# Second value head stored with its two batches exchanged, and PSUM regrouped into one quad of banks, in a gated delta rule kernel

## The chip, the cores and the metric

The kernel runs on one core of one Trainium2 chip, as one launch. The metric is the device time in microseconds (us). A core has TensorE (PE: matmuls, and PEld: its weight loads), VectorE (DVE), ScalarE (ACT), GpSimd (POOL) and DMA queues, of which SyncE (SP) issues most. Engines run their own instruction streams and meet at semaphores.

## The reference

Two independent parts. A small one (a ternary-quantised feed-forward step on tokens) is done in the first 470 us and isn't touched. The large one, cut to what matters:

```python
# x: (8, 512, 256); 16 key heads (HK), 32 value heads (HV), two value heads per key head; width 128; chunks of 64 tokens
q, k, v, z = split(x @ W_qkvz)                      # per key head: q 128, k 128, v 2*128, z 2*128
q, k, v = silu(causal_conv1d([q, k, v], 4 taps))
# per value head: g cumulative decay within a chunk, A = -(beta k) k^T * exp(g_i - g_j), strictly lower
attn = (I - A)^-1                                    # _correct_row, done by rows in the reference
value_corrected = attn @ (v * beta);  k_cumdecay = attn @ (k * beta * exp(g))
for c in range(8):                                   # chunks
    v_prime = value_corrected[c] - k_cumdecay[c] @ state
    out[c] = (q_c @ state) * exp(g) + tril(q_c k_c^T * decay) @ v_prime
    state = state * exp(g_last) + (k_c * k_decay)^T @ v_prime
y = rmsnorm(out * silu(z)) @ W_out
```

## The kernel before

Batches are taken two at a time (NB = 2, four pairs), and for each pair the 16 key heads in turn: 64 steps, called heads here, numbered g. A head carries its two value heads (h = 0, 1) together. A tile of 128 partitions is 64 tokens of batch 0 above 64 tokens of batch 1 (`half(b)`), so a product of one batch's chunk uses a quarter of TensorE's array: rows `half(b)` by columns `half(b)`, given by `tile_position`.

The kernel is a software pipeline written by hand. `core` of head g walks its 8 chunks (c = 0..7), and into it `weave` sets the 24 pieces of `front` of head g+1 (`front_piece`, s = 0..23, three per chunk). Each engine has its own version of both, and the order in them is the order of issue. On TensorE one chunk is `core_step`: `key_state` (state times keys), `query_state`, `out_project` of chunk c-3, `output_rows` (transposes of chunk c-2), piece 3c, `solve` (inverse times residual), piece 3c+1, `update` (state products), `intra`, piece 3c+2. ScalarE copies `solve`'s result to `ww`, VectorE forms `residual` and `update_state` (four scalar_tensor_tensor of 128x128), `gate_out` multiplies by silu(z).

The front projects the next head through a ring of two PSUM banks (`pj`), in the order k, k, z, q, q, v0, z, v0, k transposed (kt) twice, v1, v1, z, z, v transposed (vt) four times. `fill_ring(n)` on TensorE waits until `pcopy` says that entry n-2 has been emptied by ScalarE's `empty_ring`. So the second q (n = 4, in piece 5) waits for the first z (n = 2). Behind that second q stand, in piece 5, `square_sums` (L673) and `chunk_squares` (L687). The inverse is made by small blocks: VectorE inverts 16x16 blocks (`invert_rows` to `join_right`), DMAs put them in place (`dd`, `ee` and, for the second head's turned half, `eturn`), TensorE does `off_products` and three `fixpoint` rounds of 64x64 products, ScalarE negates (`negated`), VectorE adds (`add_round`).

PSUM has the banks pj0, pj1, ms0, ms1 (front), `dsb` (two banks: state products, transposed rows, output projection), `pot` (key_state and solve) and `pod` (query_state and intra).

## Time and profile before

| | us |
|---|---|
| median of 3 runs | 4962.62 (4961.70 to 4965.15) |
| the profiled execution | 4955.99 |
| its span, first to last instruction | 4954.2 |
| TensorE busy | 4628.7 (93%) |
| VectorE busy | 3573.7 (72%) |
| ScalarE busy | 3072.0 (62%) |
| GpSimd busy | 694.4 (14%) |
| mean granted TensorE clock | 0.986 |

The profile is one execution. Its parts are the busy times, the span in 40 slices, the queues, the chain that ended last, the groups of instructions by line, and the DMA issues. Further views are asked of the same trace: a timeline (instructions of one engine in order, neighbours of the same line merged, start and length in us, with idle time and its releaser in brackets), groups by line and shape, and sums by stretch. The matmuls' ends are modelled and overlap the next start, so the time that a group of matmuls holds TensorE is read from its start to the next group's start. A float32 product shows as two MATMUL records, a transpose as one.

### The profile page before, as it was taken

Reading aid. Unit: us, or ns where it says so; the run is one execution under the profiler, and the core shown is the slowest. Engines: PE = TensorE matmul, PEld = TensorE weight load, DVE = VectorE, ACT = ScalarE, POOL = GpSimd, SP = SyncE. Lnnn points to the kernel's source line nnn. Section 1 sums busy time; section 2 is a strip of 40 time slices with the busy share of each in tenths; the row PEclk is TensorE's granted clock in tenths of the full one; section 3 lists DMA queues with packets and bytes.
Section 4 is the critical chain, followed back from the end, with each engine's and each line's share of the span. In section 5 each row is a group of like instructions: output and inputs, shape, how many; then the busy total and the mean of one; then the engine's idle time right before and its main releaser. Section 6 shows DMA issues by size and latency. Waiting matters only on the chain.

```text
span 4954.2 us, 144941 instructions
## 1 busy us (share of the span) xinstructions
PE 4628.7 (93%) x54288; PEld 3167.2 (64%) x54320; DVE 3573.7 (72%) x7576; ACT 3072.0 (62%) x7979; POOL 694.4 (14%) x680
## 2 busy tenths in 40 slices
PE   4998999999999899999999899999999899999998
PEld 2555666666666566666666566666666666666666
DVE  7554677777777677777777677777777677777776
ACT  2333666666666566666666566666666566666665
POOL 0000111111111111111111111111111111111111
PEclk8999999999999999999999999999999999999999
DMA  2111222222223222222223222222223222222221
GB/s 61 41 35 63 63 69 55 60 66 61 68 56 77 66 69 53 61 66 61 69 50 79 69 61 56 65 66 62 56 60 82 68 59 58 64 67 61 69 59 34
DMA packets 760100, 305.22 MB, mean 62 GB/s; under 512 B 672880, under 2 KB 716016, under 8 KB 749168
## 3 DMA queue, kind: packets, MB, share of 16 engines
q1 hardware_dynamic: 620144, 287.40, 23.5%
q10 hardware_dynamic: 139264, 8.42, 1.8%
q8 instruction: 455, 7.45, 0.6%
q14 instruction: 237, 1.94, 0.1%
HBM read 216.96 MB, written 66.07 MB: 57 GB/s over the span
## 4 chain that ended last, share of the span: by engine, by line
issue 56%; PE 27%; POOL 8%; DVE 4%; ACT 2%; DMA 1%; SPq 1%; POOLq 0%; DVEq 0%; ACTq 0%
PE pj L660 5%; POOL rout L1559 4%; PE dsb L819 3%; PE pj L655 2%; POOL gb L1550 2%; POOL kn L1555 2%; PE pot L605 2%; PE dsb L791 1%; PE pot L777 1%; PE ms L693 1%; PE pod L803 1%; PE ms L589 1%; PE pot L748 1%; PE pj L589 1%; PE pod L760 1%
## 5 line engine op out<-in xcount | busy, mean ns | idle before, releaser
L660 PE MATMUL pj<-xnT,wt 128*128 128x512 f32 x2048 | 1022.2, 622 | 34.0 <-DMA cw<-in_L_attn_conv_weight 20.6
L1292 DVE SCALAR_TENSOR_TENSOR cy<-xpad,cw,cy 128x1024 f32<-128x1024 f32 x768 | 976.2, 1278 | 7.9 <-ACT cy L1003 0.9
L1559 POOL TENSOR_TENSOR rout<-rin,expo 128x2 f32<-128x2 f32 x512 | 358.3, 700 | 3737.4 <-DVE rin L1443 3737.4
L1429 DVE SCALAR_TENSOR_TENSOR st<-st,gel,dsb 128x128 f32<-128x128 f32 x1536 | 430.9, 343 | 288.0 <-PE dsb L791 285.1
L819 PE MATMUL dsb<-wo,yT 128*128 128x256 f32 x2048 | 575.0, 403 | 13.2 <-issue 12.1
L660 PEld LDWEIGHTS pj<-xnT,wt 128*128 128x128 f32 x2048 | 351.7, 191 | 363.8 <-issue 349.0
L1002 ACT ACTIVATE xpad<-pj 128x512 f32<-128x512 f32 x512 | 305.5, 597 | 359.1 <-PE pj L660 359.1
L655 PE MATMUL pj<-wt,xnT 128*128 128x256 f32 x2048 | 509.9, 392 | 0.0
L1062 ACT ACTIVATE yT<-dsb 128x256 f32<-128x256 f32 x512 | 203.2, 397 | 469.0 <-PE dsb L810 467.5
L819 PEld LDWEIGHTS dsb<-wo,yT 128*128 128x128 f32 x2048 | 348.0, 189 | 117.8 <-issue 89.6
L655 PEld LDWEIGHTS pj<-wt,xnT 128*128 128x128 f32 x2048 | 368.3, 189 | 84.6 <-issue 44.3
L791 PEld LDWEIGHTS dsb<-ww,arena 64*128 64x128 f32 x3584 | 234.9, 186 | 274.0 <-issue 269.9
L994 ACT ACTIVATE arena<-pj 128x512 f32<-128x512 f32 x256 | 153.1, 598 | 392.2 <-issue 247.8
L1057 ACT ACTIVATE arena<-arena,rout 128x128 f32<-128x128 f32 x1024 | 352.6, 395 | 59.0 <-POOL rout L1559 55.7
L1416 DVE SCALAR_TENSOR_TENSOR rr<-pot,nge,arena 128x128 f32<-128x128 f32 x896 | 270.5, 343 | 115.8 <-PE pot L748 115.8
L1051 ACT ACTIVATE junk<-arena 128x128 f32<-128x128 f32 x1024 | 315.3, 324 | 57.2 <-DVE arena L1439 49.9
L1003 ACT ACTIVATE cy<-pj,cw 128x512 f32<-128x512 f32 x512 | 350.2, 684 | 0.0
L803 PE MATMUL pod<-ww,arena 64*64 64x128 f32 x4096 | 334.9, 281 | 13.7 <-ACT ww L1045 10.4
L791 PE MATMUL dsb<-ww,arena 64*128 64x128 f32 x3584 | 320.5, 297 | 8.3 <-issue 4.2
L777 PE MATMUL pot<-rr,bda 64*64 64x128 f32 x3584 | 293.5, 282 | 19.0 <-DVE rr L1416 19.0
L748 PE MATMUL pot<-st,kq 128*64 128x256 f32 x1792 | 289.8, 398 | 6.1 <-DVE st L1429 4.6
L760 PE MATMUL pod<-st,qge 128*64 128x128 f32 x3584 | 276.9, 273 | 3.2 <-issue 3.2
(174 smaller groups left out, 8009.7 us busy)
## 6 DMA issues: line engine op xcount, KB each, us to landing
qge<-ge_rows SPq DMA_DIRECT2D x64, 1024.0 KB, 7.1
wt<-in_L_attn_W_qkvz SPq DMA_DIRECT2D x64, 768.0 KB
gb<-g_rows SPq DMA_DIRECT2D x128, 256.0 KB
a_d<-at SPq DMA_DIRECT2D x64, 512.0 KB, 2.6
wo<-in_L_attn_W_out SPq DMA_DIRECT2D x64, 256.0 KB, 2.7
x_d<-xpair SPq DMA_DIRECT2D x128, 128.0 KB, 1.8
ap_<-a_d SPq DMA_DIRECT2D x512, 16.0 KB, 1.8
dd<-x_d SPq DMA_DIRECT2D x512, 16.0 KB, 2.1
```

Of the source, the lines that this page charges most:

```text
L655: last = mm(pj[n % 2][:, v * GRP * DH:(v + 1) * GRP * DH], xnT[:, k, c * P:(c + 1) * P], wt[:, k, 4 * DH:4 * DH + GRP * DH], start=(k == 0 ...
L660: last = mm(pj[n % 2][:, :], wt[:, k, col:col + DH], batch(xnT, k, i), start=(k == 0), stop=(k == KD - 1))
L748: last = mm(pkw[half(b), 0:GRP * DH], kq[:, p, c, b, :], st[:, c % 2, b, :, :].rearrange("p h d -> p (h d)"), start=True, stop=True, tile_ ...
L777: last = mm(pkw[half(b), (GRP + h) * DH:(GRP + h + 1) * DH], bda[half(b), p, c * GRP + h, :], rhs, start=True, stop=True, tile_position=(b ...
L791: last = mm(dsb[:, b, h * DH:(h + 1) * DH], kkd[p][half(b), c * GRP + h, :], ww[half(b), h, :], start=True, stop=True, tile_position=(b * ...
L803: last = mm(po[half(b), h * DH:(h + 1) * DH], it[half(b), p, c * GRP + h, :], ww[half(b), h, :], start=(c == 0), stop=True, skip_group_che ...
L819: last = mm(dsb[:, 0, GRP * DH:GRP * DH + D], yT[:, h, :], wo[:, p, h, :], start=(h == 0), stop=(h == GRP - 1))
L1003: last = fn(cy[:, m % 2, i, :], src[:, :], ACT.Copy, scale=cw[:, m, TAPS - 1:TAPS])
L1057: last = fn(zz[p][:, j, h, :], zz[p][:, j, h, :], ACT.Copy, scale=rout[:, h:h + 1])
L1292: stt(y, x[:, :, tap:tap + SEQ], cw[:, kind, tap:tap + 1], y, ALU.mult, ALU.add).then_inc(S["conv"], 1)
L1429: last = stt(st[:, (c + 1) % 2, b, h, :], st[:, c % 2, b, h, :], gel[:, p, h, b * NC + c:b * NC + c + 1], dsb[:, b, h * DH:(h + 1) * DH], ...
L1559: tt(rout[:, :], rin[:, :], expo[:, 0, 0:GRP], ALU.pow).then_inc(S["routs"], 1)
```

## The change

All of one kind: value head 1 is kept with its batches exchanged, so that its batch 0 lies in partitions 64 to 127 (`home(b, h)`).

- `solve` and `intra` now place their four products on the four quarters of the array, two heads by two batches, where before both heads used the same two quarters one after the other. The two heads' results go to different banks (`po` in banks 0 and 1 of `quad`, `pw` in banks 1 and 2).
- `key_state` is four products of 128 columns, for two of 256.
- Rows per value head come head by head (h, c) where they came chunk by chunk (c, h), in `g_rows`, `cols`, `kkd`, `vb`, `bda`, `it`.
- ScalarE exchanges z's second head as it empties the ring: three SILU instructions (128x256 for head 0, two of 64x256 that cross the partition halves for head 1) for one of 128x512. For the first z (n = 2) the one of head 0 stands where it was, and the two of head 1 stand behind `silu` and `squares` of k; only they add to `pcopy`. v transposed is emptied by four 128x128 with the key norm as scale, for two of 128x256.
- `output_rows` undoes the exchange: an ordinary float32 matmul against an identity shifted by 64 for head 1, for a transpose.
- `fixpoint` rounds 0 and 2 take the second head from the straight product; round 0 waits for the third negation and no longer for `eturn`, which VectorE's `add_round(0, 1)` now waits for. `add_round(0, .)` moves from piece 20 to chunk 7 behind `residual(7)`; `decayed_squares(1)` from chunk 6 ahead of `mean_square` to the end of chunk 5; one `convolve` from piece 17 to 18.
- `intra(7)` waits also for `accumulate`, and chunk 0 begins with a wait for the head before's last `gate_out`.
- `update_state` stays four scalar_tensor_tensor, now from banks 2 and 3 of `quad`. The z products and the output projection stay as they are on TensorE, but for the bank.

```diff
-        dsb = ctx.enter_context(nc.psum_tensor("dsb", [P, NB, 512], F32))
...
+        quad = ctx.enter_context(nc.psum_tensor("quad", [P, 4, 512], F32))
+        pot, pod, pch, pds = (quad[:, n, :] for n in range(4))
+        po = quad[:, 0:2, DH:2 * DH]
+        pod_rows = quad[:, 0, 2 * DH:2 * DH + D]
+        pw = quad[:, 1:3, 0:DH]
+        pks = quad[:, 2, 0:GRP * DH]
+        pyt = quad[:, 3, 0:GRP * DH]
+        pstate = quad[:, 2:4, GRP * DH:2 * GRP * DH]
...
+        def home(b, h):
+            return b if h == 0 else 1 - b
...
             def key_state(g, p, c):
-                for b in range(NB):
-                    last = mm(pkw[half(b), 0:GRP * DH], kq[:, p, c, b, :],
-                              st[:, c % 2, b, :, :].rearrange("p h d -> p (h d)"), start=True, stop=True,
-                              tile_position=(0, b * CH))
+                for h in range(GRP):
+                    for b in range(NB):
+                        last = mm(pks[half(b), h * DH:(h + 1) * DH], kq[:, p, c, home(b, h), :],
+                                  st[:, c % 2, home(b, h), h, :], start=True, stop=True, tile_position=(0, b * CH))
...
             def solve(g, p, c):
-                for h in range(GRP):
-                    for b in range(NB):
-                        rhs = rr[half(b), h, :] if c else vb[p][half(b), h, :]
-                        last = mm(pkw[half(b), (GRP + h) * DH:(GRP + h + 1) * DH], bda[half(b), p, c * GRP + h, :],
-                                  rhs, start=True, stop=True, tile_position=(b * CH, b * CH))
+                for a in range(NB):
+                    for h in range(GRP):
+                        rhs = rr[half(a), h, :] if c else vb[p][half(a), h * NC, :]
+                        last = mm(pw[half(home(a, h)), h, :], bda[half(a), p, h * NC + c, :], rhs,
+                                  start=(c == 0 or h == 1), stop=True, skip_group_check=True,
+                                  tile_position=(a * CH, home(a, h) * CH))
...
             def intra(g, p, c):
-                if c == 0:
-                    before(pe, "og", g)
                 if c == NC - 1:
                     after(pe, "wev", g, NC)
+                    after(pe, "accs", g, c - 3 + 1)
-                        last = mm(po[half(b), h * DH:(h + 1) * DH], it[half(b), p, c * GRP + h, :], ww[half(b), h, :],
-                                  start=(c == 0), stop=True, skip_group_check=True, tile_position=(b * CH, b * CH))
+                        last = mm(po[half(home(b, h)), h, :], it[half(b), p, h * NC + c, :], ww[half(b), h, :],
+                                  start=(c == 0), stop=True, skip_group_check=True,
+                                  tile_position=(b * CH, home(b, h) * CH))
...
             def output_rows(g, p, j):
-                    last = tp(dsb[:, 1, (GRP + h) * DH:(GRP + h + 1) * DH], zz[p][:, j, h, :], ident)
+                    last = mm(pyt[:, h * DH:(h + 1) * DH], zz[p][:, j, h, :], cst[:, h * CH:h * CH + P],
+                              start=True, stop=True)
...
-            def empty_ring(g, p, n):
+            def empty_ring(g, p, n, part=None):
...
-                    for v in range(2):
-                        c = 2 * i + v
-                        last = fn(vb[p][:, c * GRP:(c + 1) * GRP, :].rearrange("p h d -> p (h d)"),
-                                  src[:, v * GRP * DH:(v + 1) * GRP * DH], ACT.Copy, scale=kn[:, c:c + 1])
+                    for v in range(4):
+                        c, h = 2 * i + v // GRP, v % GRP
+                        last = fn(vb[p][:, h * NC + c, :], src[:, v * P:(v + 1) * P], ACT.Copy, scale=kn[:, h, c:c + 1])
                 elif kind == "z":
-                    last = fn(zz[p][:, 2 * i:2 * i + 2, :, :].rearrange("p c h d -> p (c h d)"), src[:, :], ACT.Silu)
+                    z = src[:, :].rearrange("p (c h d) -> p c h d", c=2, h=GRP)
+                    if part != 1:
+                        last = fn(zz[p][:, 2 * i:2 * i + 2, 0, :], z[:, :, 0, :], ACT.Silu)
+                    if part != 0:
+                        for b in range(NB):
+                            last = fn(zz[p][half(1 - b), 2 * i:2 * i + 2, 1, :], z[half(b), :, 1, :], ACT.Silu)
+                    if part == 0:
+                        return
...
                 for n in range(RING):
                     if s == slots[n]:
                         if n == 3:
                             silu(g, p, 0)
                             squares(g, p, 0)
-                        empty_ring(g, p, n)
+                            empty_ring(g, p, 2, 1)
+                        empty_ring(g, p, n, 0 if n == 2 else None)
...
             def fixpoint(g, p, r):
                 if r == 0:
                     loaded(pe, d_ee, g, GRP * NBLK)
-                    loaded(pe, d_et, g, GRP * NBLK)
-                    after(pe, "pneg", g, 2)
+                    after(pe, "pneg", g, 3)
```

ScalarE, chunk 1, piece 4, where the ring's entries 2 (z) and 3 (q) are emptied. Names: arena holds z, the squares and most head data; `kq` is the convolved k; `xpad`, `cy` take a projection for the convolution. Before:

```order
L994 ACT_TABLE_LOAD
L994 ACTIVATE arena<-pj 128x512
L247 REGISTER_ALU
L251 ISA
L1016 ACTIVATE kq<-cy 128x2x8x64
L247 REGISTER_ALU
L251 ISA
L1023 ACTIVATE arena<-kq 128x1024
L247 REGISTER_ALU
L1002 ACTIVATE xpad<-pj 128x512
L1003 ACTIVATE cy<-pj,cw 128x512
```

And after:

```order
L1005 ACT_TABLE_LOAD
L1005 ACTIVATE arena<-pj 128x2x128
L251 REGISTER_ALU
L255 ISA
L1033 ACTIVATE kq<-cy 128x2x8x64
L251 REGISTER_ALU
L255 ISA
L1040 ACTIVATE arena<-kq 128x1024
L1008 ACTIVATE arena<-pj 64x2x128 x2
L251 REGISTER_ALU
L1019 ACTIVATE xpad<-pj 128x512
L1020 ACTIVATE cy<-pj,cw 128x512
```

The z entry was emptied by one instruction ahead of k's silu; now its last two instructions stand behind silu and squares.

TensorE, the same chunk, with the semaphores that each piece waits for (`quad` is the new PSUM tensor). Before:

```order
L777 MATMUL pot<-rr,bda 64x128 [waits rs_]
L777 MATMUL pot<-rr,bda 64x128 x3
L660 MATMUL pj<-xnT,wt 128x512 [waits pcopy]
L660 MATMUL pj<-xnT,wt 128x512
L791 MATMUL dsb<-ww,arena 128x128 [waits wev]
L791 MATMUL dsb<-ww,arena 128x128 x3
L803 MATMUL pod<-ww,arena 64x128 x4
L660 MATMUL pj<-xnT,wt 128x512 [waits pcopy]
L660 MATMUL pj<-xnT,wt 128x512
L673 MATMUL ms<-ones,arena 64x1 [waits sqs,yadd]
```

And after:

```order
L777 MATMUL quad<-rr,bda 64x128 [waits rs_]
L777 MATMUL quad<-rr,bda 64x128 x3
L668 MATMUL pj<-xnT,wt 128x512 [waits pcopy]
L668 MATMUL pj<-xnT,wt 128x512
L792 MATMUL quad<-ww,arena 128x128 [waits wev]
L792 MATMUL quad<-ww,arena 128x128 x3
L803 MATMUL quad<-ww,arena 64x128 x4
L668 MATMUL pj<-xnT,wt 128x512 [waits pcopy]
L668 MATMUL pj<-xnT,wt 128x512
L681 MATMUL ms<-ones,arena 64x1 [waits sqs,yadd]
```

Nothing moved here: the second projection (the second q) stands behind `intra` and waits for the same count of `pcopy`, which the z entry now adds later.

## Rows read from the trace of the kernel before

**Rows 1.** The page, part 1: busy time, share, instructions.

```profile
PE 4628.7 (93%) x54288; PEld 3167.2 (64%) x54320; DVE 3573.7 (72%) x7576; ACT 3072.0 (62%) x7979; POOL 694.4 (14%) x680
```

**Rows 2.** Sums by stretch: start:end, length, each engine's busy time, PEclk, DMA share, GB/s.

```profile
542.00:1610.00 1068.00, 1031.37 (x12660) 709.63 (x12659) 801.00 (x1738) 713.66 (x1886) 162.69 (x156) 1.00 0.27 63
```

**Rows 3.** Groups by line and shape: count, busy us, mean ns, idle before and releasers.

```profile
L803 PE MATMUL pod<-ww,arena 64*64 64x128 f32 x4096 | 334.9, 281 | 13.7 <-ACT ww L1045 10.4 <-issue 3.3
L810 PE MATMUL dsb<-cst,arena 128*128 128x128 f32 x1024 | 196.3, 274 | 0.0
L994 ACT ACTIVATE arena<-pj 128x512 f32<-128x512 f32 x256 | 153.1, 598 | 392.2 <-issue 247.8 <-PE pj L655 136.7
```

**Rows 4.** Timeline of TensorE in chunk 1 of one head: start us, length us, instruction.

```profile
2549.99 0.65 PE L748 MATMUL pot<-st,kq 128*64 128x256 f32 x4
2550.47 0.61 PE L760 MATMUL pod<-st,qge 128*64 128x128 f32 x8
...
2551.97 0.38 PE L810 MATMUL dsb<-cst,arena 128*128 128x128 f32 x2
2552.28 0.65 PE L777 MATMUL pot<-rr,bda 64*64 64x128 f32 x8
2552.87 1.99 PE L660 MATMUL pj<-xnT,wt 128*128 128x512 f32 x4
2554.78 0.72 PE L791 MATMUL dsb<-ww,arena 64*128 64x128 f32 x8
2555.43 0.65 PE L803 MATMUL pod<-ww,arena 64*64 64x128 f32 x8
2556.01 1.98 PE L660 MATMUL pj<-xnT,wt 128*128 128x512 f32 x4
2558.22 0.48 PE L673 MATMUL ms<-ones,arena 128*64 128x1 f32 x11 [0.22 <-ACT arena L1023]
```

**Rows 5.** TensorE, off_products: four quarters in turn, then two quarters.

```profile
2528.30 1.16 PE L693 MATMUL ms<-dd,off 64*64 64x64 f32 x64 [0.51 <-DVE arena L1339]
2529.25 1.14 PE L693 MATMUL pj<-dd,off 64*64 64x64 f32 x32
2530.32 0.71 PE L791 MATMUL dsb<-ww,arena 64*128 64x128 f32 x8
```

**Rows 6.** Timeline of ScalarE in the same chunk as rows 4.

```profile
2552.99 0.39 ACT L1045 ACTIVATE ww<-pot 128x256 f32<-128x256 f32 x1 [0.21 <-PE pot L777]
2553.27 0.68 ACT L1057 ACTIVATE arena<-arena,rout 128x128 f32<-128x128 f32 x2
...
2555.26 0.60 ACT L994 ACTIVATE arena<-pj 128x512 f32<-128x512 f32 x1
2555.76 1.05 ACT L1016 ACTIVATE kq<-cy 128x1024 f32<-128x1024 f32 x1
2556.92 1.06 ACT L1023 ACTIVATE arena<-kq 128x1024 f32<-128x1024 f32 x1
2557.88 0.58 ACT L1002 ACTIVATE xpad<-pj 128x512 f32<-128x512 f32 x1
```

**Rows 7.** ScalarE: v transposed emptied (128x256), k transposed emptied (128x128).

```profile
2539.22 1.57 ACT L991 ACTIVATE arena<-pj,kn 128x256 f32<-128x256 f32 x4 [0.98 <-PE pj L650]
...
2574.95 4.24 ACT L983 ACTIVATE arena<-pj,ckd 128x128 f32<-128x128 f32 x16
```

**Rows 8.** Sums by stretch, columns as rows 2, around two idle times of TensorE.

```profile
3940.00:3943.40 3.40, 1.40 (x10) 0.97 (x8) 2.24 (x6) 0.00 (x0) 0.70 (x1) 1.00 0.13 12
3943.40:3946.80 3.40, 3.40 (x76) 2.88 (x76) 0.42 (x1) 2.18 (x5) 0.00 (x0) 0.50 0.86 253
2320.00:2323.30 3.30, 1.21 (x74) 1.11 (x69) 0.88 (x1) 1.78 (x4) 0.12 (x1) 1.00 0.61 147
2323.30:2327.00 3.70, 3.70 (x115) 3.30 (x116) 2.15 (x6) 2.20 (x6) 0.00 (x0) 1.00 0.25 97
```

**Rows 9.** VectorE, end of chunk 0: the first state, which key_state of chunk 1 waits for.

```profile
2548.91 0.68 DVE L1434 COPY st<-dsb 128x512 f32<-128x512 f32 x1
```

**Rows 10.** TensorE, first product of fixpoint round 0.

```profile
2532.31 0.24 PE L693 MATMUL ms<-ee,pbd 64*64 64x64 f32 x1 [0.69 <-DMA eturn<-x_d]
```

**Rows 11.** Weight loads (PEld) of the output projection, by line.

```profile
L819 PEld LDWEIGHTS dsb<-wo,yT 128*128 128x128 f32 x2048 | 348.0, 189 | 117.8 <-issue 89.6 <-ACT yT L1062 1.5
```

More of the change, by code:

```diff
@@ L39 @@
 RING = PROJ_TILES + 6
-IDENT, CAP, SCANMASK = 0, P, P + CH
+IDENT, CAP = 0, P + CH
+SCANMASK = CAP + CH
 CONSTS = SCANMASK + SEQ
@@ L759, in query_state @@
                     for b in range(NB):
-                        last = mm(po[half(b), h * DH:(h + 1) * DH],
-                                  qge[:, p, h, c * P + b * CH:c * P + (b + 1) * CH],
-                                  st[:, c % 2, b, h, :], start=(h == 0), stop=False, skip_group_check=True,
-                                  tile_position=(0, b * CH))
+                        row = c * P + home(b, h) * CH
+                        last = mm(po[half(b), h, :], qge[:, p, h, row:row + CH], st[:, c % 2, home(b, h), h, :],
+                                  start=True, stop=False, skip_group_check=True, tile_position=(0, b * CH))
                 last.then_inc(S["qs"], 1)
@@ L818, in out_project @@
                 for h in range(GRP):
-                    last = mm(dsb[:, 0, GRP * DH:GRP * DH + D], yT[:, h, :], wo[:, p, h, :],
-                              start=(h == 0), stop=(h == GRP - 1))
+                    last = mm(pod_rows, yT[:, h, :], wo[:, p, h, :], start=(h == 0 and not bank_cleared),
+                              stop=(h == GRP - 1), skip_group_check=True)
                 last.then_inc(S["od"], 1)
@@ L849, in core_step @@
                     query_state(g, p, c)
+                else:
+                    before(pe, "og", g)
                 two, three = behind(g, p, c, 2, first), behind(g, p, c, 3, first)
                 if three:
-                    out_project(*three)
+                    out_project(*three, c > 0)
                 if two:
@@ L933, in column_stage @@
                 for b in range(NB):
-                    fn(colstage[half(b), :, i, :].rearrange("p k (c h) -> p k c h", h=GRP),
-                       src[:, b], ACT.Copy).then_inc(colev, 1)
+                    dst = colstage[half(b), :, i, :].rearrange("p k (h c) -> p k c h", h=GRP)
+                    if i < COLS - 1:
+                        last = fn(dst, src[:, b], ACT.Copy)
+                    else:
+                        for h in range(GRP):
+                            last = fn(dst[:, :, :, h], src[:, home(b, h), :, :, h], ACT.Copy)
+                    last.then_inc(colev, 1)
             def aside(q, t, place):
@@ L1001, in empty_ring @@
                             loaded(act, d_w, g, 4)
-                    fn(xpad[:, m % 2, i, TAPS - 1:], src[:, :], ACT.Copy)
-                    last = fn(cy[:, m % 2, i, :], src[:, :], ACT.Copy, scale=cw[:, m, TAPS - 1:TAPS])
+                    place = 1 - i if kind == "v1" else i
+                    fn(xpad[:, m % 2, place, TAPS - 1:], src[:, :], ACT.Copy)
+                    last = fn(cy[:, m % 2, place, :], src[:, :], ACT.Copy, scale=cw[:, m, TAPS - 1:TAPS])
                 last.then_inc(S["pcopy"], 1)
@@ L1317, in query_eps @@
                 after(dve, "sskq", g, 2)
-                ts(qe[:, p, :], ms[1][:, NC:2 * NC], L2_EPS, RMS_EPS * DH, ALU.add, ALU.mult).then_inc(S["coef"], 1)
+                for b in range(NB):
+                    ts(qe[half(1 - b), p, 1, :], ms[1][half(b), NC:2 * NC], L2_EPS, RMS_EPS * DH, ALU.add, ALU.mult)
+                ts(qe[:, p, 0, :], ms[1][:, NC:2 * NC], L2_EPS, RMS_EPS * DH, ALU.add, ALU.mult).then_inc(S["coef"], 1)
             def scale_decay(g):
@@ L1403, in add_round @@
                 src = ms[n][:, :].rearrange("p (u c) -> p u c", u=8)
-                add = eturn[:, :, :] if (r, n) == (1, 1) else ee[:, us, :]
+                if (r, n) == (0, 1):
+                    loaded(dve, d_et, g, GRP * NBLK)
+                add = eturn[:, :, :] if n and r != 1 else ee[:, us, :]
                 if r < 2:
```

97 lines of the change are left out of this document (46 added, 51 removed).

## Prediction, written before the changed kernel was timed

> **What bounds the kernel now.** First the busy times: TensorE 93%, VectorE 72%, ScalarE 62% [rows 1]. The share is an average, so next the sums by stretch. From 542 to 1610 us, some fifteen heads, TensorE is busy for 1031 of 1068 us [rows 2]. L803 has 4096 records at 8 for a chunk, so 512 chunks or 64 heads [rows 3]; the stretch gives about 68.2 us for a head (68.0 to 68.3 in a look at several), of which TensorE waits some 2.5 us. So a microsecond saved on TensorE counts where nothing else is late, and a wait added to it counts in full. Third, the timeline of one chunk on TensorE and ScalarE side by side [rows 4, 6]: TensorE goes from group to group with one wait of 0.22 us, for ScalarE's squares. That is the place to look at: ScalarE, with 62% on average, runs without a gap from 2555.26 to 2558.4 us there, since it has emptied z, done silu and squares and only then q.
>
> **TensorE's own work.** The time of a group is start to next start.
> - solve takes 2552.87 - 2552.28 = 0.59 us, intra 2556.01 - 2555.43 = 0.58 [rows 4]. Each has four pair-steps of 128 columns. What four quarters give instead of two is in off_products: 64 products of 64 columns on four quarters take 0.95 us, the next 32 on two quarters 1.07 us [rows 5], so 15 ns each against 33: twice the throughput. A pair-step of 128 columns costs about 0.11 us: a projection's four passes of 512 columns take 2554.78 - 2552.87 = 1.91 us, 0.12 for 128 columns with the group's fixed time in it [rows 4], and four steps of 0.11 leave solve a fixed 0.15. Two of four pair-steps go: 0.22, less 0.01 for the longer first step, 0.21 us. 16 groups a head: -3.3 us. Ends: 0 (no more overlap at 128 columns) and -3.5.
> - output_rows: two transposes take 2552.28 - 2551.97 = 0.31 us, with the fixed 0.1. A transpose is one record (1024 for 512 chunks, two each) [rows 3], a float32 product two; so two passes more, each 128 columns, 0.11 each: +0.22 a chunk, +1.75 a head. Ends: +0.22, and +0.45 a chunk if each of the four passes is held by its own weight load, which the rows show at 189 ns for float32 [rows 11] (4 x 0.189 - 0.31). I take the lower, since loads are issued while the pass before runs.
> - The Trainium skill (TensorE: Matmul & The Clock Gate, section LDWEIGHTS) puts a load at columns / 1.2 ns, 107 ns for 128 columns, whatever the rows. By it the load hides under the pass and the term is +0.22; by the 189 ns of the row it would be +0.45, 118 us more in all. The row's length may hold latency that overlaps.
> - key_state: four products of 128 for two of 256, the same columns: 0 to +0.05 a chunk. I take 0.
>
> Sum if nothing else were late: -1.55 us a head.
>
> **The z entry of the ring.** This decides. The second q (the projection at 2556.01) [rows 4] may start once the first z has been emptied. Now ScalarE starts that at 2555.26, frees the bank at 2555.86, and TensorE, there at 2556.01, has no wait. After the change, counted from the start of z: head 0's half 0.28 us (the step of a 128x256 copy: L1045 at 2552.99, next at 2553.27) [rows 6]; silu from 0.28 to 1.33; squares from 1.44 to 2.50, the next instruction 0.96 after it starts (2556.92 to 2557.88) [rows 6], so at 2.40; two instructions of head 1, 0.28 and 0.38 us: freed at 3.06, seen by TensorE at 3.13. TensorE is there at 0.75 - 0.20 (intra is shorter; solve is shorter for both) = 0.55. So **2.6 us of wait in every head**, in order, with nothing to overtake it: square_sums, chunk_squares, key_state(2) and VectorE's coefficients stand behind it. It takes up the 0.2 us of wait that L673 had [rows 4]: +2.4 net. Ends: +2.0 to +2.8 (copy step against Silu step for the half entries).
>
> **Other waits.**
> - v transposed: four 128x256 take 1.57 us, 0.39 each; sixteen 128x128 of the k entry take 4.24, 0.265 each [rows 7]. An entry goes from 0.79 to 1.06 us. The fourth entry then waits for the second to be emptied (start + 0.83, + 2.12): about +0.45 a head. The squares behind them come 0.9 us later, and with them VectorE's mean_square, decayed queries, and the first state, which now lands at 2549.6 against a use at 2549.99 [rows 9, 4]: slack 0.4, so +0.25.
> - Where TensorE gets early and finds another engine: before the second L673 (chunk 3), where ScalarE's silu and squares set the time, intra's 0.2 is lost; chunks 4 and 5 run up to VectorE's join_right and the DMAs behind it, 0.35 is lost; chunk 6 likewise 0.2: +0.75.
> - The wait of fixpoint round 0 for eturn (0.69 us here, 0.5 us a head) [rows 10] goes, and off_products' 0.51 us behind decayed_squares [rows 5] too. What is late next is the third negation on ScalarE: it ended on average 1 us before that fixpoint started, and the two z entries ahead of it are 0.35 us longer each (0.84 for 0.49). I give -0.3. Against it VectorE's two add_rounds and a convolve more stand ahead of round 1: +0.2 at worst, taken as +0.1.
>
> **Sum for a head:** -1.55 + 2.4 + 0.45 + 0.25 + 0.75 - 0.3 + 0.1 = +2.1; I take +2.0, since c = 1's intra is counted on both sides. 63 woven heads: +126 us. On the profiled execution, 4955.99, that is 5082; the median lies 6.6 us above it, so 5089.
>
> **The clock.** From 3940.0 to 3943.4 us TensorE was busy for 1.40 us, and the next 3.4 us ran at 0.50, which is 1.2 of 2.4 GHz; from 2320.0 to 2323.3 it was busy for 1.21, and the clock stayed at 2.4 [rows 8]. In both it waited once for some 2 us. The new wait of 2.6 us is longer, so either can follow it. 3.4 us at half clock hold back 1.7 us of work. If every second new wait brings one: 63 / 2 x 1.7 = +54 us. The Trainium skill (TensorE: Matmul & The Clock Gate, The HAM clock gate) says that throttled is the default and activity releases it; that gives no other number here.
>
> Likeliest: 5089 + 54 = 5143, rounded to **5140 us**, 3.6% slower.
>
> **Rivals.**
> 1. The wait stands, the clock holds: 5089. For it: the rows of 2320 us. Against: those of 3940. Chance 0.2.
> 2. The clock falls after every new wait, or for two stretches each: 5089 + 107 = 5196, up to 5300. For it: after the long waits of several microseconds it stayed low for two stretches. Chance 0.13.
> 3. Faster: the second q is not held, because the z entry is freed in time. That needs ScalarE to reach z in chunk 1 at least 2.6 us earlier against TensorE than now; between ww at 2552.99 and z at 2555.26 lie a scaling of 0.7 us and 1.28 us of table load [rows 6], and nothing in the change takes these away. It decides at a wait below about 0.4 us a head. Then the sum is 2.0 - 2.4 - 0.1 = -0.5 us a head, 4931. With every other gain kept too (no lost 0.75) it is 4884. Chance 0.08.
> 4. The change doesn't do what it says: four quarters don't overlap at 128 columns with two banks. Then +3.3 comes back, less what the waits absorb (about 0.8): +2.5 x 63 = +158, 5300. Against it: rows 5. Chance 0.05.
> 5. Near no change: the z wait is half as long and the waits at the head's end don't appear: about 4965. Chance 0.04.
>
> **How the numbers follow.** The likeliest case has 0.5. Its own range, from the ends of the z wait (-0.4 to +0.4 us, 25 us either way), of the clock (a third to two thirds of the heads, 18 us) and of the absorbed gains (0.5 us, 30 us), is 5085 to 5195. To hold 8 in 10 I take rivals 1 and most of 2: 5020 to 5220. What a measurement of this kernel can tell from no change is about 0.2%, 10 us. Slower: 0.5 + 0.2 + 0.13 + 0.05 = 0.88; within 0.2%: 0.04; faster: 0.08.
>
> **What the profile after would show.** The projection ahead of the first square sums with an idle time of 2.6 us, released by ScalarE's z line; solve and intra at 0.37 to 0.38 us from start to next start; output_rows at 0.53; the fourth v entry with 0.4 us of idle time; stretches at 0.50 clock in many heads shortly behind that projection, none of them in the middle before; L673's wait for the squares gone; the wait for eturn on TensorE gone. Wrong: if that projection starts within 0.5 us of intra's end, the main term falls and rival 3 holds; if solve stays at 0.58, rival 4.

## The result, and the profile after

The changed kernel takes 5261.37 us (median of 4 runs, 5246.43 to 5265.44), against 4962.16 us for the kernel before on the same chip: ratio 1.060, 95% interval 1.058 to 1.062. It is slower by 299 us, where 178 were predicted, and lies above the predicted range. The span of its profiled execution is 5257.7 us, 303.5 more than before. Here and below, four executions that ran throughout at a lower granted clock than the others (0.66 to 0.92 in the mean) are left out of the times and ratios.

First the page's part 1 of the kernel after (it answers to rows 1), then its sums by stretch from 542 to 1610 us (rows 2):

```profile
PE 4725.6 (90%) x57104; PEld 3286.2 (63%) x57136; DVE 3610.7 (69%) x7832; ACT 3302.4 (63%) x9011; POOL 767.1 (15%) x680
```

```profile
542.00:1610.00 1068.00, 981.12 (x12377) 686.61 (x12375) 750.96 (x1659) 711.58 (x1970) 169.07 (x144) 0.96 0.25 57
```

TensorE was idle for 37 of these 1068 us, and is now for 87; the granted clock in the stretch fell from 1.00 to 0.96. The waits by releaser, TensorE, from 542 us to the end (us in total, times, longest), first two of the kernel before that the kernel after doesn't have:

```profile
PE ms L693 <- DMA eturn<-x_d: 24.1, 28, 1.4
PE ms L693 <- DVE arena L1339: 24.0, 43, 0.7
```

And the five longest of the kernel after:

```profile
PE pj L668 <- ACT arena L1008: 172.9, 63, 3.7
PE ms L701 <- issue: 39.9, 69, 2.0
PE ms L701 <- DMA dd<-x_d: 27.2, 35, 1.4
PE ms L681 <- ACT arena L1040: 21.1, 63, 0.5
PE quad L750 <- DVE st L1456: 17.0, 38, 1.7
```

One wait stands far above the others: 172.9 us in 63 heads, 2.74 each, of the projection L668 for ScalarE's L1008, the second head's half of z. The timeline of TensorE in chunk 1 of one head, as rows 4:

```profile
2695.34 0.61 PE L811 MATMUL quad<-cst,arena 128*128 128x128 f32 x4
2695.88 0.45 PE L777 MATMUL quad<-rr,bda 64*64 64x128 f32 x8
2696.25 1.98 PE L668 MATMUL pj<-xnT,wt 128*128 128x512 f32 x4
2698.17 0.71 PE L792 MATMUL quad<-ww,arena 64*128 64x128 f32 x8
2698.81 0.45 PE L803 MATMUL quad<-ww,arena 64*64 64x128 f32 x8
2702.01 1.98 PE L668 MATMUL pj<-xnT,wt 128*128 128x512 f32 x4 [2.75 <-ACT arena L1008]
```

Solve (L777 to L668) takes 0.37 us from start to next start, it was 0.59; output_rows (L811 to L777) 0.54, it was 0.31. Both groups are as predicted. Then TensorE stands idle for 2.75 us. ScalarE meanwhile, as rows 6:

```profile
2698.66 0.38 ACT L1005 ACTIVATE arena<-pj 128x256 f32<-128x256 f32 x1
2698.95 1.05 ACT L1033 ACTIVATE kq<-cy 128x1024 f32<-128x1024 f32 x1
2700.11 1.06 ACT L1040 ACTIVATE arena<-kq 128x1024 f32<-128x1024 f32 x1
2701.19 0.77 ACT L1008 ACTIVATE arena<-pj 64x256 f32<-64x256 f32 x2
2701.98 0.60 ACT L1019 ACTIVATE xpad<-pj 128x512 f32<-128x512 f32 x1
```

It holds one bank of the ring from 2698.66 to 2701.96, since silu (L1033) and squares (L1040) stand between z's two halves.

What follows such a wait: sums by stretch around another head's, whose projection started at 847.53 (columns as rows 2), and that projection in the timeline.

```profile
843.90:847.30 3.40, 0.89 (x16) 0.52 (x14) 1.55 (x6) 3.24 (x6) 0.00 (x0) 1.00 0.00 0
847.30:850.70 3.40, 3.17 (x4) 1.18 (x4) 0.00 (x0) 1.36 (x3) 0.00 (x0) 0.51 0.02 5
850.70:854.10 3.40, 3.40 (x82) 2.90 (x82) 1.61 (x9) 1.75 (x6) 0.00 (x0) 0.99 0.00 0
```

```profile
847.53 3.57 PE L668 MATMUL pj<-xnT,wt 128*128 128x512 f32 x4 [2.75 <-ACT arena L1008]
```

Four records (two products) that take 1.98 us at full clock take 3.57 at half (0.51 granted, 1.2 of 2.4 GHz). The clock records of the trace hold 372 us at half clock behind 542 us, against 44 us before, and some of it falls into 55 of the 63 woven heads. In 47 of the 63 heads a stretch of half clock begins within 3 us of the end of the long wait; these hold 294 of the 372 us. The Trainium skill (TensorE: Matmul & The Clock Gate, HAM oscillation) tells of a kernel in which the wait for a DMA in each step makes the clock fall in each step; the trace agrees in those 47 heads, with a wait for ScalarE, and not in the other 16.

For the account by place, the median time from one landmark to the next over heads 3 to 62 ("undisturbed": only heads without half clock, 54 before and 8 after; medians, so the rows don't add up exactly to the period):

```
stretch, us                                undisturbed: before  after   change
first to second square sums (L673 / L681)               17.08   16.93    -0.15
to join_right (VectorE)                                 11.98   12.44    +0.46
to fixpoint round 0                                     13.41   12.84    -0.57
to v transposed                                          5.83    5.93    +0.10
to the next output projection                            3.05    3.80    +0.75
to key_state of chunk 1                                  8.55    8.90    +0.35
to the second q projection                               6.03    8.66    +2.63
to the next square sums                                  2.20    1.91    -0.29
period                                                  68.30   71.64    +3.34
period, mean over all these heads                       69.47   74.06    +4.59
```

So, of the 303.5 us, 63 x 3.34 = 210 come without any half clock, and 63 x (4.59 - 3.34) = 79 with it; the last 14 lie outside the woven heads. Eight heads are few: the 44 undisturbed heads of e2 below, where the wait for z is filled with useless work and the period should be the same, have 71.31 us, which would put 20 us less in the first term and as much more in the second. The experiments price the places.

The same undisturbed heads, divided into the time that TensorE holds (start to next start, less idle time) and its idle time, medians a head:

```
us a head                       before  after   change   predicted
held by TensorE's own work       66.25  65.51    -0.74       -1.55
idle, the wait for z              0.00   2.75    +2.75       +2.6
idle, all the rest                2.11   3.26    +1.15       +1.05
```

The predicted 1.05 are the prediction's +0.75, +0.45, +0.25, -0.3 and +0.1, less the 0.2 us that L673 no longer waits.

### The profile page after: what moved, and what is told of

The parts are those of the page before. It is cut to its first block, busy times and chain, and to the rows that moved or that the text cites. A ratio compares the mean times of both kernels' runs of the same rounds, so it can differ in the third digit from the quotient of the medians.

```text
span 5257.7 us, 151813 instructions
## 1 busy us (share of the span) xinstructions
PE 4725.6 (90%) x57104; PEld 3286.2 (63%) x57136; DVE 3610.7 (69%) x7832; ACT 3302.4 (63%) x9011; POOL 767.1 (15%) x680
## 4 chain that ended last, share of the span: by engine, by line
issue 59%; PE 15%; POOL 9%; DVE 8%; ACT 6%; DMA 1%; ACTq 1%; SPq 0%; POOLq 0%; DVEq 0%
POOL rout L1585 4%; POOL kn L1580 3%; POOL gb L1575 2%; PE pj L668 2%; PE quad L613 2%; PE quad L821 1%; PE ms L597 1%; ACT arena L993 1%; PE pj L597 1%; DVE qge L1366 1%; PE ms L701 1%; PE pj L663 1%; PE quad L750 1%; ACTq L341 1%; DVE cy L1308 1%
## 5 line engine op out<-in xcount | busy, mean ns | idle before, releaser
L668 PE MATMUL pj<-xnT,wt 128*128 128x512 f32 x2048 | 1086.2, 656 | 196.5 <-ACT arena L1008 177.6
L668 PEld LDWEIGHTS pj<-xnT,wt 128*128 128x128 f32 x2048 | 369.6, 201 | 550.7 <-issue 356.6
L821 PE MATMUL quad<-wo,yT 128*128 128x256 f32 x2048 | 580.8, 406 | 11.9 <-issue 10.4
L1451 DVE SCALAR_TENSOR_TENSOR st<-st,gel,quad 128x128 f32<-128x128 f32 x1536 | 429.8, 342 | 205.9 <-PE quad L792 205.7
L821 PEld LDWEIGHTS quad<-wo,yT 128*128 128x128 f32 x2048 | 353.0, 192 | 121.2 <-issue 91.5
L792 PEld LDWEIGHTS quad<-ww,arena 64*128 64x128 f32 x3584 | 238.4, 189 | 273.2 <-issue 268.8
L1438 DVE SCALAR_TENSOR_TENSOR rr<-quad,nge,arena 128x128 f32<-128x128 f32 x896 | 270.4, 343 | 128.7 <-PE quad L750 128.7
L1001 ACT ACTIVATE arena<-pj,kn 128x128 f32<-128x128 f32 x1024 | 277.3, 392 | 91.3 <-PE pj L658 90.3
L792 PE MATMUL quad<-ww,arena 64*128 64x128 f32 x3584 | 325.0, 300 | 7.0 <-ACT ww L1062 4.4
L750 PE MATMUL quad<-st,kq 128*64 128x128 f32 x3584 | 304.6, 291 | 26.1 <-DVE st L1456 17.0
L811 PEld LDWEIGHTS quad<-cst,arena 128*128 128x128 f32 x2048 | 310.7, 192 | 27.3 <-issue 0.3
L811 PE MATMUL quad<-cst,arena 128*128 128x128 f32 x2048 | 312.7, 275 | 0.0
```

What stands on the lines that cost most here:

```text
L668: last = mm(pj[n % 2][:, :], wt[:, k, col:col + DH], batch(xnT, k, i), start=(k == 0), stop=(k == KD - 1))
L750: last = mm(pks[half(b), h * DH:(h + 1) * DH], kq[:, p, c, home(b, h), :], st[:, c % 2, home(b, h), h, :], start=True, stop=True, tile_pos ...
L792: last = mm(pstate[:, b, h * DH:(h + 1) * DH], kkd[p][half(b), h * NC + c, :], ww[half(b), h, :], start=True, stop=True, tile_position=(b ...
L811: last = mm(pyt[:, h * DH:(h + 1) * DH], zz[p][:, j, h, :], cst[:, h * CH:h * CH + P], start=True, stop=True)
L821: last = mm(pod_rows, yT[:, h, :], wo[:, p, h, :], start=(h == 0 and not bank_cleared), stop=(h == GRP - 1), skip_group_check=True)
L1451: last = stt(st[:, (c + 1) % 2, b, h, :], st[:, c % 2, b, h, :], gel[:, p, h, b * NC + c:b * NC + c + 1], pstate[:, b, h * DH:(h + 1) * DH ...
```

## Experiments

Each experiment was timed together with further runs of the kernel before. Kernels are compared by their ratios to it, times 4962 us; what such a difference can be off by is given where it matters (95%).

**e1: z emptied whole ahead of silu.** In `front_piece` of ScalarE:

```diff
                             squares(g, p, 0)
-                            empty_ring(g, p, 2, 1)
-                        empty_ring(g, p, n, 0 if n == 2 else None)
+                        empty_ring(g, p, n)
```

> The changed kernel, with the first z entry emptied whole (three instructions) ahead of k's silu and squares. Theory W (the wait of the second q for the z entry, 2.75 us in each of 63 heads, with the half-clock stretches that follow it, is the main cost): the wait falls to about 0.45 us and 0.2 us comes back before the square sums, -1.9 us a head or -120, and the half-clock stretches shrink to those of the kernel before (45 us from 370), worth another 80 to 110: 5030 to 5060. Rival L (the load that the change puts on ScalarE, VectorE and the extra passes on TensorE are the cost, wherever they stand): within 1% of the changed kernel, above 5200.

Measured: 5032.71 us, ratio 1.0136 (1.0102 to 1.0170): 230 us (211 to 249) of the 299 are gone by moving two short instructions. The wait, and the projection's group, from the waits and from the groups by shape of e1:

```profile
PE pj L668 <- ACT arena L1008: 40.0, 63, 1.6
```

```profile
L668 PE MATMUL pj<-xnT,wt 128*128 128x512 f32 x2008 | 996.0, 619 | 48.9 <-ACT arena L1008 40.0 <-DMA cw<-in_L_attn_conv_weight 8.9
```

The wait lost 133 us; half clock fell from 372 to 83 us. The mean of one record is 619 ns; in the kernel after it is 654 over the same stretch, and 620 before. 133 us of wait, less the 16 us by which L681's wait for ScalarE grew (21.1 to 37.5), and 0.30 x 289 = 87 us of clock, by the price that e2 gives, make 204 of the 230.

**e2: the wait filled with work.** The long wait stays, but TensorE is kept busy in it: five products of 256 columns whose result nobody reads, ahead of the second q.

```diff
+                        if n == 4:
+                            before(pe, "yadd", g)
+                            apart(pe)
+                            for _ in range(5):
+                                mm(ms[0][:, 0:256], wt[:, 0, 0:DH], xnT[:, 0, 0:256], start=True, stop=True)
                         fill_ring(g, p, n, hk == 0)
```

> The changed kernel, with five products of 256 columns (results unused) issued on TensorE just ahead of the second q, 2.15 us of work inside its wait of 2.75 us. Nothing else moves, so this prices the clock alone. Theory W: half-clock stretches after 542 us fall from 372 us to under 100, and the time by 90 to 165: 5100 to 5170. Rival (the clock falls for another reason, the half-clock time overlaps other waits and costs nothing): 5240 to 5270.

Measured: 5175.41 us, ratio 1.0426 (1.0390 to 1.0462), just above the range of theory W. From key_state of chunk 1 to the second q it still is 8.66 us in the median, but half clock falls from 372 to 89.5 us. So the clock alone is worth (1.0599 - 1.0426) x 4962 = 86 us (65 to 107), 0.30 us (0.23 to 0.38) for each microsecond at half clock. Useless work that nothing waits for made the kernel 1.6% faster.

**e3: the rows turned by a transpose.** The identity may be shifted for a transpose too:

```diff
-                    last = mm(pyt[:, h * DH:(h + 1) * DH], zz[p][:, j, h, :], cst[:, h * CH:h * CH + P],
-                              start=True, stop=True)
+                    last = tp(pyt[:, h * DH:(h + 1) * DH], zz[p][:, j, h, :], cst[:, h * CH:h * CH + P])
```

> The changed kernel, with output_rows made by a transpose against the same shifted identity, one pass in place of two. Theory W takes the two further passes as 0.22 us in each of 512 chunks, on the path: -0.22 x 512 = -113, 5150. Rival (they are absorbed by waits for ScalarE that come later): above 5220.

Measured: 5207.81 us, ratio 1.0482 (1.0443 to 1.0521), 58 us (36 to 79) less than the kernel after, half of the 113 that two passes a chunk are worth; theory W had 113, the rival under 40. Its waits, TensorE:

```profile
PE pj L668 <- ACT arena L1007: 172.9, 63, 3.7
PE quad L777 <- DVE rr L1437: 46.2, 132, 0.5
```

The second line is new: solve waits for VectorE's residual for 46.2 us, where the kernel after has 4.1. A good part of what TensorE saves, it waits.

**e11: the reverse, in the kernel before.** There the same rows are turned by a matmul:

```diff
-                    last = tp(dsb[:, 1, (GRP + h) * DH:(GRP + h + 1) * DH], zz[p][:, j, h, :], ident)
+                    last = mm(dsb[:, 1, (GRP + h) * DH:(GRP + h + 1) * DH], zz[p][:, j, h, :], ident, start=True, stop=True)
```

> The kernel before with one edit: the output rows are turned by a matmul against the identity, as the kernel after turns them, and no longer by a transpose; a correct kernel. TensorE's own work grows by 2 x 0.11 us in each of 512 chunks, 113 us. Theory F (before the change TensorE is late nearly everywhere and every term of its own work counts in full, which is how the prediction took it): 5065 to 5085 us. Theory H (as in the kernel after, where taking it away was worth 53 us: TensorE is waited for in about half of the chunks only): 5010 to 5040 us.

Measured: 5059.63 us, ratio 1.0194 (1.0173 to 1.0215), +96 us, 0.19 us a chunk, just under the expected range of theory F (5065 to 5085). Groups by shape of e11, from 542 us on:

```profile
L810 PE MATMUL dsb<-cst,arena 128*128 128x128 f32 x2048 | 312.3, 275 | 0.0
L777 PE MATMUL pot<-rr,bda 64*64 64x128 f32 x3584 | 293.0, 282 | 3.8 <-DVE rr L1416 3.6
```

Two records for each of the rows, each of 275 ns as the one of a transpose [rows 3]; and solve's wait for the residual shrinks from 18.6 us before to 3.6. Work added to TensorE is paid nearly in full (96 of 113), the same work taken away gives half (58 of 113).

**e4: z late in the kernel before.** One line of order: z's one instruction behind silu and squares.

```diff
                         if n == 3:
                             silu(g, p, 0)
                             squares(g, p, 0)
+                            empty_ring(g, p, 2)
```

and `n == 2` is skipped at its own place.

> The kernel before, with one thing of the change: its first z entry, still one instruction, is emptied behind k's silu and squares. Theory W: the bank is freed 2.8 us after z's start was, TensorE is there at 0.75, so it waits 2.05 us less the 0.2 that it waited later: +117, and the clock falls after a part of these waits, +30 to +90: 5110 to 5170. Rival L: 4960 to 4990.

Measured: 5271.39 us, ratio 1.0617 (1.0582 to 1.0652), +306 us: 100 us above the expected range, and not a clean test. ScalarE in one head of e4:

```profile
2709.44 0.38 ACT L1045 ACTIVATE ww<-pot 128x256 f32<-128x256 f32 x1 [0.21 <-PE pot L777]
2709.72 0.68 ACT L1057 ACTIVATE arena<-arena,rout 128x128 f32<-128x128 f32 x2
2711.67 1.28 ACT L1016 ACT_TABLE_LOAD   x1 [1.26 <-DVE cy L1295]
2712.96 1.06 ACT L1016 ACTIVATE kq<-cy 128x1024 f32<-128x1024 f32 x1
2714.13 1.06 ACT L1023 ACTIVATE arena<-kq 128x1024 f32<-128x1024 f32 x1
2715.09 0.58 ACT L994 ACTIVATE arena<-pj 128x512 f32<-128x512 f32 x1
```

The table load stands in front of the first instruction that needs it. That was z, which waited for nothing; now it is silu, which waits 1.26 us for VectorE's convolution, and the load waits with it. Silu, squares and z all come 1.25 us later. (Trainium skill, ScalarE: Activation LUTs, What ACT_TABLE_LOAD costs: a load of 1283 ns and a drain of some 1380. The load agrees, 1.28 us; of the drain the rows show nothing: silu starts 0.01 us after the load ends, and in the kernel after the load starts 0.02 us behind the instruction before it.)

**e5: the same place, with the table load kept early.** In the kernel before, z is emptied by head, 128x256 each, head 0 at its place, head 1 behind silu and squares; no batches are exchanged.

```diff
+                    if part is None:
+                        last = fn(zz[p][:, 2 * i:2 * i + 2, :, :].rearrange("p c h d -> p (c h d)"), src[:, :], ACT.Silu)
+                    else:
+                        last = fn(zz[p][:, 2 * i:2 * i + 2, part, :], z[:, :, part, :], ACT.Silu)
...
                             squares(g, p, 0)
-                        empty_ring(g, p, n)
+                            empty_ring(g, p, 2, 1)
+                        empty_ring(g, p, n, 0 if n == 2 else None)
```

> The kernel before with one edit: z's first projection tile is emptied by head, head 0 where the whole tile was, head 1 behind silu and squares; no batches are exchanged. The table load then stays where it is (ahead of head 0's half), which was what spoilt the former run with z late. Theory W (this place alone costs what it cost in the kernel after, whatever the rest does): the wait of the second q tile is about 2.4 us (2.75 less the second of two short entries), 1.7 to 2.0 us more per head than before, about +115 us, and the half clock that came with the wait in the kernel after (290 us of stretch more than with z emptied whole, worth some 90 us) comes too: 5150 to 5200 us. Theory C (the clock falls in the kernel after because of the sum of its many small waits): about +115 us and hardly more half clock than before, 5070 to 5100 us. Theory N (the wait is taken out of waits that stand later anyway): under 5040 us.

Measured: 5149.84 us, ratio 1.0384 (1.0352 to 1.0415), +190 us (175 to 206). Waits of TensorE in e5:

```profile
PE pj L660 <- ACT arena L998: 125.8, 63, 2.7
```

2.0 us in each of 63 heads, where 2.4 were expected, and 265 us at half clock for 44. Less the 0.2 us a head that L673 no longer waits, that is 125.8 - 12.6 + 0.30 x 221 = 180 us, within the interval. So this one placement explains its cost without any of the rest, and theory C (the sum of many small waits lets the clock fall) is out.

**e6: query_eps moved.** Kernel after, VectorE:

```diff
                 if s == 12:
-                    query_eps(g, p)
                     invert_rows(g, 5, 8)
...
                 if s == 17:
+                    query_eps(g, p)
                     decayed_squares(g, p, 1)
```

VectorE's timeline in the kernel after shows what stood there, three instructions for the one of before, in front of the small inverse that everything behind join_right waits for:

```profile
2653.78 0.42 DVE L1474 TENSOR_TENSOR acc<-quad,acc 128x256 f32<-128x256 f32 x1
2654.22 0.34 DVE L1337 TENSOR_SCALAR qe<-ms 64x8 f32<-64x8 f32 x2
2654.58 0.17 DVE L1338 TENSOR_SCALAR qe<-ms 128x8 f32<-128x8 f32 x1
2654.66 0.23 DVE L1386 TENSOR_TENSOR prod<-ap_,xpair 128x50 f32<-128x50 f32 x1
```

> The kernel after with one edit: query_eps, three instructions on VectorE, stands behind join_right (piece 17) and no longer ahead of invert_rows (piece 12). Theory Q (the 0.46 us by which join_right came later is on the path): the stretch from the second square sum to join_right returns to 12.0 us, the period of a clean head is 0.3 to 0.45 us shorter, 5225 to 5245 us. Rival (join_right's result is waited for by transfers that end late only together with something else, here the third negation): the stretch shortens, the next grows by as much, 5255 to 5265 us.

Measured: 5224.44 us, ratio 1.0533 (1.0513 to 1.0553), 33 us (19 to 47) less. The stretch to join_right is 11.90 us. Three instructions on 8 columns each cost 0.5 us a head.

**e7: v in two instructions.** Kernel after; head 1 is scaled with head 0's key norms, so its own scale is left out.

```diff
-                    for v in range(4):
-                        c, h = 2 * i + v // GRP, v % GRP
-                        last = fn(vb[p][:, h * NC + c, :], src[:, v * P:(v + 1) * P], ACT.Copy, scale=kn[:, h, c:c + 1])
+                    for v in range(2):
+                        c = 2 * i + v
+                        last = fn(vb[p].rearrange("p (h c) d -> p c h d", h=GRP)[:, c],
+                                  src[:, v * GRP * P:(v + 1) * GRP * P].rearrange("p (h d) -> p h d", h=GRP),
+                                  ACT.Copy, scale=kn[:, 0, c:c + 1])
```

> The kernel after with one edit: each transposed v tile is emptied by two instructions of 128x256 as before, rather than four of 128x128. It leaves out one thing: head 1 is scaled by head 0's key norms. Theory V (the 0.75 us that the stretch from v's transpose to the next output projection grew is ScalarE's four entries): that stretch returns to 3.05 to 3.2 us, a clean head is 0.5 to 0.75 us shorter, 5210 to 5230 us. Rival (it is the longer output_rows and the later queue; the entries lie beside it): 5250 to 5262 us.

Measured: 5228.38 us, ratio 1.0539 (1.0513 to 1.0565), 30 us (14 to 46) less, 0.5 us a head. Between the output projection and key_state of chunk 1 the median is 8.36 us for 8.90. The stretch before that, from v transposed to the output projection, is 3.56 us for 3.76, but e2, where v isn't touched, has 3.55 too; so the growth of that stretch, which the expectation took for v's, isn't explained.

**e8: e1, e3 and e6 together.** The three edits above, in the kernel after.

> The kernel after with three edits, a correct kernel: z's first tile is emptied whole ahead of silu, the output rows are turned by a one-pass transpose against the shifted identity, and query_eps stands behind join_right. The first was worth 229 us alone, the second 53 us, the third is expected at 16 to 36 us. Theory A (they add): 4935 to 4965 us, about the time of the kernel before. Theory S (with the long wait gone TensorE is late nearly everywhere, so its own work counts in full, and the transpose is worth up to 113 us): 4880 to 4920 us. Theory G (what each gives is partly the same half clock, which can only be won once): 4970 to 5010 us.

Measured: 4958.66 us, ratio 1.0000 (0.9984 to 1.0015). By the ratios the three should give 230 + 58 + 33 = 321 us, that is 0.995; measured are 297 (285 to 309). They add up to within 8%, theory A. At half clock it is 123 us, for 44 before: 24 us by e2's price. Waits of TensorE in e8:

```profile
PE quad L777 <- DVE rr L1436: 53.3, 70, 1.0
PE pj L668 <- ACT arena L1007: 39.9, 63, 1.6
PE ms L681 <- ACT arena L1039: 38.4, 111, 0.5
PE ms L701 <- issue: 37.0, 67, 2.2
PE quad L750 <- DVE st L1454: 26.9, 49, 1.6
```

**e9: e8 with one convolution step moved.** In e8 most of the first wait is one of 0.8 us in nearly every head, at chunk 6. VectorE there, and TensorE:

```profile
2612.12 1.28 DVE L1306 SCALAR_TENSOR_TENSOR cy<-xpad,cw,cy 128x1024 f32<-128x1024 f32 x1
2613.31 0.61 DVE L1436 SCALAR_TENSOR_TENSOR rr<-quad,nge,arena 128x128 f32<-128x128 f32 x2
2615.26 0.16 DVE L1463 SCALAR_TENSOR_TENSOR rin<-ss,qe 128x2 f32<-128x2 f32 x1 [1.35 <-ACT junk L1066]
```

```profile
2614.06 0.45 PE L777 MATMUL quad<-rr,bda 64*64 64x128 f32 x8 [0.81 <-DVE rr L1436]
2614.80 1.16 PE L701 MATMUL ms<-dd,off 64*64 64x64 f32 x64 [0.30 <-issue]
```

The edit, besides those of e8:

```diff
+                if s == 18:
+                    convolve(g, 2, 3)
                 if s == 21:
...
-                for n, at_s in enumerate((2, 3, 3, 8, 8, 9, 15, 15, 17, 18, 18, 20)):
+                for n, at_s in enumerate((2, 3, 3, 8, 8, 9, 15, 15, None, 18, 18, 20)):
```

> The kernel of e8 (whole z first, transpose, query_eps late) with one edit more, a correct kernel: the third convolution step of v0 (1.28 us on VectorE) stands behind the residual of chunk 6 and no longer ahead of it. In the trace of e8 TensorE's solve of chunk 6 waits 0.81 us for that residual in 59 of 61 heads (47.9 us), and right behind it VectorE stands idle for 1.35 us waiting for ScalarE's output squares. Theory R (the gain of the faster parts is lost at that place): the wait goes and nothing takes its place, 4905 to 4930 us, about 0.9% under the kernel before. Rival (TensorE stands a little later for the next of VectorE's results, the sums or the state of chunk 6): 4945 to 4965 us.

Measured: 4955.77 us, ratio 0.9981 (0.9969 to 0.9992): 9 us better than e8, which isn't clear of the noise (0 to 19), and not 48. TensorE in e9 at the same place, and its waits:

```profile
2593.28 0.45 PE L777 MATMUL quad<-rr,bda 64*64 64x128 f32 x8
2595.04 1.16 PE L701 MATMUL ms<-dd,off 64*64 64x64 f32 x64 [1.31 <-DMA dd<-x_d]
```

```profile
PE ms L701 <- DMA dd<-x_d: 43.3, 44, 2.2
```

The wait for the residual is gone (53.3 us to 1.5), and the wait for the transfer of the small inverses takes most of its place (4.3 us to 43.3). Counted from the head's first square sums, off_products start at 37.5 us in e8 and at 37.1 in e9 (medians), half of the 0.8 us earlier; at fixpoint round 0, 41.3 and 41.2 us in undisturbed heads, that is gone too. Theory R fell; the rival had the right outcome and the wrong place, since it is the transfer that is late next, not VectorE's sums or state.

**e10: the same move in the kernel before.** It takes one step more along: v1's first convolution step goes from piece 17 to 18, where the kernel after has it.

> The kernel before with the same move of the convolution step, as a control for e9: there the solve waits for residuals for 18.6 us in all. Theory R: at most that much is gained, and decayed_squares already stands behind the residual of chunk 6, so that the step now delays it or what follows it: 4945 to 4975 us, no change. Rival (the move is worth in itself what it is worth in e9): 4915 to 4935 us.

Measured: 4951.14 us, ratio 0.9972 (0.9960 to 0.9984), 14 us faster than before: a small gain, inside the range of theory R and no sign of the 48 us. Which of the two moved steps gives it was not separated. It is the best kernel of the study; e9 with all of the exchange is no better (0.9981).

## Why the prediction was wrong, step by step

- **The z wait: right.** 2.6 us predicted, 2.75 measured; less the 0.2 us that L673 no longer waits, +2.5 for +2.4. (The table's +2.63 and -0.29 also hold what solve, intra and output_rows changed in these stretches.) Its cause and price are shown three times: by e1 (-230 us), by e5 (+190 us in the kernel before) and by the waits.
- **TensorE's own work (-1.55): right for each group, too good in the sum, the first step that failed.** Solve 0.37, intra shorter alike, output_rows +0.22 with the lower end for the transposes' replacement; but the time that TensorE holds in a head fell by 0.74 us only (0.73 in the 43 undisturbed heads of e1). Most chunks are 0.18 shorter, as predicted. The one with fixpoint round 1 is 0.40 longer, 6.79 us for 6.39. There solve and the products of rounds 1 and 2 together hold TensorE for 2.7 us before and after, though solve alone was to save 0.2; the transposes of v take 0.2 us more, which the prediction had at nothing; and the longer output_rows comes on top. In the kernel before, a part of the free quarters was in use there already:

```profile
2535.95 0.54 PE L777 MATMUL pot<-rr,bda 64*64 64x128 f32 x5
2536.23 0.27 PE L693 MATMUL ms<-at,pback 64*64 64x64 f32 x1
2536.34 0.27 PE L777 MATMUL pot<-rr,bda 64*64 64x128 f32 x1
```

  Round 1 (L693) starts 0.28 us behind solve's first product and runs between its last ones; after the change it starts 0.64 us behind it. That this is why nothing was saved there is argued from these rows, not shown by an experiment.
- **Gains lost where TensorE gets early (+0.75): right in kind, and in size as far as the waits tell.** All idle time but z's grew by 1.15 us a head where the prediction's terms give 1.05 (of the measured, up to 0.5 is the next point). e3 and e11 show such a loss by one and the same piece of work: 0.19 us a chunk when added, 0.11 when taken away; and e9 shows at one place how: what TensorE gains before off_products goes to a wait for VectorE's residual or, if that is taken away, mostly for the DMA. In e8 TensorE has 2.5 us less own work a head than before, and the undisturbed period is 68.1 for 68.3 us. Idle time ahead of the 64x64 products with no releaser in the trace ("issue", 39.9 us for 22.7 before) is a part of it that stays open.
- **query_eps: missed.** The prediction didn't cost two more VectorE instructions of 0.17 us, nor the later end of join_right: +0.46 us in the table, 33 us by e6.
- **v transposed (+0.45) and the state (+0.25): about right, in part in another place.** e7 prices the entries at 0.5 us a head; the wait for the state is 17.0 / 63 = 0.27 us. The wait expected at the fourth v entry isn't the main thing (L658 waits for ScalarE in 20 heads only, 7.6 us in all); key_state of chunk 1 and the output projection come later.
- **The fixpoint (-0.3): right in kind, too small.** -0.57; the transfer eturn is no longer waited for, and the third negation is next, 0.1 us ahead of the fixpoint in the median where it was 1.2.
- **The clock (+54): mis-sized, the second step that failed.** "Every second new wait brings one" of 3.4 us: measured are 47 of 63 behind the long wait, often with 6.8 or 10.2 us, and 328 us more at half clock in all. Against it, a microsecond at half clock costs 0.30 us and not 0.5, probably since TensorE waits in part of it anyway, which no run here shows by itself. Together 86 us by e2, 79 by the table: 25 to 32 us more than predicted. The row of 3940 us [rows 8] was the right witness, that of 2320 the exception.
- **Sum:** a head takes 3.34 us more for +2.0, 84 us in all, of which TensorE's own work has 0.8 us a head or 50 us; with 25 us of the clock and some 14 outside the woven heads that makes up about the 121 us between 178 and 299. Of the other 34 us, z and the other waits have 0.1 to 0.2 us a head each; the rest is the rounding of the prediction's 2.1 to 2.0 and what medians of eight heads leave over.
- **Rivals.** 2 (the clock falls after nearly each wait) is nearest, and the time lies in its range: its mechanism held in three heads of four at a lower price, and the base was higher, so a part of that match is luck. 1 fell by the clock's records, 3, 4 and 5 by the timeline: the bank is held, the quarters overlap.

## What to carry to other kernels

Ask of each entry of a ring what stands between its first and its last instruction: two short instructions behind two long ones cost 230 us of 5261, more than a third of it (0.30 x 289 = 87 us) by the clock that fell behind the wait. Add up what a change saves over the whole period, not at one clean place: in the one chunk where solve already ran beside other products, nothing was gained. In this kernel, with TensorE at 93%, a piece of work taken away gave half of its time (e3) and the same piece added cost nearly all of it (e11); so look up the next wait before counting a gain in full. Count instructions on the second engine too: three that touch eight columns each cost 0.5 us a head where they stood ahead of a chain that others wait for.

## What the runs showed of the hardware

- Behind a single wait in each period of about 72 us, half clock began in 47 of 63 heads, with 2.75 us (the kernel after) as with 2.0 us (e5); behind waits of 0.6 us at the same place (e1) in 1 of 63, and with the wait filled by useless products (e2) in none.
- A float32 transpose against an identity shifted by 64 columns gives the exchanged rows, in one record of 274 ns; the ordinary float32 product takes two of 275.
- ScalarE's table load of 1.28 us waits with the instruction that it stands in front of (e4): an instruction that waits for nothing, set ahead, takes the load before the wait.
